# Layer-norm statistics as columns, with routing and replication interleaved

## The reference

```
xn = (x - mean(x)) / sqrt(var(x) + 1e-5)
attn: q, k, v = xn @ w_qkv.T + b; q = silu(q); k = softmax(k, over tokens)
      out = q @ (k.T @ v) per head; out = layernorm(out) * sigmoid(gate(xn)); out @ w_out.T + b_out
ffn:  logits = xn @ Wr.T                  # 8 experts, the two best per token
      w = softmax(top two); a token is dropped where its place in the expert's queue is 769 or more
      out = sum over the two of w * (xn @ We[e])
```

## Time and profile before

| what | before |
|---|---|
| median of 6 runs | 1111.31 us (1108.59 to 1203.64) |
| the profiled execution | 1109.03 us |
| its span on the slowest core (core 5) | 1107.2 us (1102.3 to 1107.2 over the cores) |
| mean granted clock of TensorE | 0.874 on core 5 |
| TensorE busy | 877.2 us, 79% of the span |
| VectorE busy | 462.4 us, 42% |
| ScalarE, GpSimd busy | 103.7 us, 53.8 us |

### The profile page before, as it was taken

The page is one execution under the profiler, slowest core; times in us unless marked ns, Lnnn a source line. Parts: engine busy times, 40 slices in busy tenths (PEclk is TensorE's granted clock), DMA queues, the critical chain, the costliest instruction groups (busy, mean ns, idle before and its releaser), DMA issues.

```text
span 1107.2 us, 11179 instructions; the slowest of 8 cores (1102.3 to 1107.2 us)
## 1 busy us (share of the span) xinstructions
PE 877.2 (79%) x3914; PEld 357.5 (32%) x3914; DVE 462.4 (42%) x700; ACT 103.7 (9%) x123; POOL 53.8 (5%) x50
## 2 busy tenths in 40 slices
PE   1446129999869986415559999999999999999992
PEld 0112003333363331101013344444444444444441
DVE  3547770033320026376763334444444444444441
ACT  1310002210003211402210000000000000000000
POOL 1000000000000000000000000000000000000244
PEclk9768559999959995755559999999999999999996
DMA  4781100050040040000000050405040505050376
GB/s 117 188 154 9 38 1 1 1 77 1 5 73 1 1 68 9 0 0 1 0 0 1 1 77 1 76 1 77 1 76 1 77 1 77 1 76 1 97 245 228
DMA packets 22149, 51.40 MB, mean 46 GB/s; under 512 B 4624, under 2 KB 4624, under 8 KB 21072
## 3 DMA queue, kind: packets, MB, share of 16 engines
q0 software_dynamic: 15008, 25.49, 15.3%
q1 hardware_dynamic: 4208, 12.63, 4.0%
q10 hardware_dynamic: 2880, 12.58, 2.9%
HBM read 67.79 MB, written 8.39 MB: 69 GB/s over the span
## 4 chain that ended last, share of the span: by engine, by line
PE 65%; DVE 19%; DMA 10%; issue 3%; ACT 2%; DVEq 1%; POOLq 0%; POOL 0%; ACTq 0%; SPq 0%
PE PS L167 65%; DVE ar L177 6%; DMA y<-fpool 6%; DVE scr_b L177 5%; DMA fpool<-x_fm 3%; DVE srow L177 3%; DVE reps L177 1%; ACT bpool L184 1%; DVE qrow L177 1%; ACT qrow L184 1%; DVEq L176 1%; DVE crow L177 0%; DVE drow L177 0%; DVE bpool L177 0%; DVE fpool L177 0%
## 5 line engine op out<-in xcount | busy, mean ns | idle before, releaser
L167 PE MATMUL PS<-ar 128*128 128x512 bf16 (+1 forms) x3200 | 705.0, 378 | 21.3 <-DVE ar L177 8.4
L167 PEld LDWEIGHTS PS<-ar 128*128 128x128 bf16 x3200 | 303.3, 100 | 387.0 <-issue 57.5
L177 DVE SCALAR_TENSOR_TENSOR ar<-PS,lc,ar 128x512 bf16<-128x512 f32 x256 | 192.1, 750 | 251.1 <-PE PS L167 251.1
L177 DVE CAST ar<-PS 128x512 bf16<-128x512 f32 x96 | 66.4, 692 | 94.1 <-PE PS L167 90.5
L167 PE MATMUL PS<-ar,ones_c_b 128*1 128x512 bf16 x64 | 22.8, 493 | 51.0 <-ACT bpool L184 50.6
L184 ACT ACTIVATE ar<-PS 128x512 bf16<-128x512 f32 x64 | 38.2, 597 | 94.7 <-PE PS L167 94.7
L167 PE MATMUL PS<-bpool,wg_sb 64*128 64x512 bf16 x32 | 18.7, 584 | 28.3 <-DVE ar L177 28.3
L198 POOL DMA_DIRECT2D ar<-we x8 | 7.0, 873 | 670.3 <-PE PS L167 670.3
L167 PE MATMUL PS<-drow,ones_b 1*128 1x512 bf16 x8 | 4.4, 554 | 44.1 <-DVE crow L177 35.2
L191 POOL TENSOR_TENSOR fpool<-ar,fpool 128x1024 f32<-128x1024 bf16 x16 | 34.2, 2136 | 90.8 <-DVE ar L177 59.7
L167 PE MATMUL PS<-bias_b,ones_b 1*128 1x512 bf16 x96 | 37.3, 389 | 0.0
(11 more groups left out here) (109 smaller groups left out, 300.0 us busy)
## 6 DMA issues: line engine op xcount, KB each, us to landing
ar<-we POOLq DMA_DIRECT2D x8, 2048.0 KB, 17.0
fpool<-x_tm SPq DMA_DIRECT2D x16, 512.0 KB, 4.1
y<-fpool ACTq DMA_DIRECT2D x16, 512.0 KB, 4.2
fpool<-x_fm SPq DMA_DIRECT2D x4, 1024.0 KB, 6.9
fpool<-x_fm ACTq DMA_DIRECT2D x4, 1024.0 KB, 6.4
ar<-wk_t POOLq DMA_DIRECT2D x1, 2048.0 KB, 23.7
ar<-wv_t POOLq DMA_DIRECT2D x1, 2048.0 KB, 17.3
ar<-wq_t POOLq DMA_DIRECT2D x1, 2048.0 KB, 16.9
```

Of the source, the lines that this page charges most:

```text
L167: i = eng.matmul(out, l, r, start=start, stop=stop)
L177: getattr(eng, name)(*a, **k).then_inc(S["dv"], 1)
```

## The change

Three new tiles: a 128x128 identity in bf16 (`ident_b128`, one more DMA on POOL's queue, ahead of the biases and the weights) and two `[128, 16]` bf16 tiles `rb_c` and `nmb_c`.

The row arithmetic of lines 287 to 312 goes. In its place TensorE first turns `srow` and `qrow` themselves into columns, in fp32, and the mean, variance, root and reciprocal are computed on `[128, 16]`. To get the rows back for the replication, the two column tiles are transposed by a matmul with the identity to `[16, 128]`, copied to SBUF, and two DMAs on SP's queue flatten them to `drow` and `crow` on one partition. All of this stands between the routing matmuls in program order: the columns ahead of chunk 0, the transposes and the DMAs ahead of chunk 2, the replication ahead of chunk 4.

```
+                w("tensor", "dv", t_stats_ev)
+                for tc in range(NT):
+                    mm(bank(4)[:, tc:tc + 1], srow[0:1, 128 * tc:128 * (tc + 1)],
+                       ones_c_f[0:1, 0:1], start=True, stop=True)
...
+                w("vector", "pe", t_cols_pe)
+                dve("tensor_scalar_mul", dsc[:], bank(4)[:, 0:NT], 1.0 / D, inc=False)
+                t_ce = dve("tensor_scalar_mul", nv1c[:], bank(4)[:, NT:2 * NT], 1.0 / D)
...
+                t_mu2 = act("activation", w0c[:], dsc[:], AF.Square)
...
+                t_csd = act("activation", v0c[:], w1c[:], AF.Sqrt, bias=eps_sb[:, 0:1])
+                w("vector", "ac", t_csd)
+                dve("reciprocal", r_c[:], v0c[:], inc=False)
+                dve("tensor_copy", rb_c[:], r_c[:], inc=False)
...
                 for h in range(HC):
+                    if h == 2:
+                        w("tensor", "dv", t_colmath)
+                        w("tensor", "d2", t_ltri)
+                        mm(bank(5)[0:16, 0:128], rb_c[:, :], ident_b128[:, :],
+                           start=True, stop=False)
+                        mm(bank(5)[0:16, 128:256], nmb_c[:, :], ident_b128[:, :],
+                           start=False, stop=True, inc=True)
...
+                        t_stg = dve("tensor_copy", bpool2[0:16, 0, 0:256],
+                                    bank(5)[0:16, 0:256])
+                        w("sync", "dv", t_stg)
+                        dma("d1", drow[0:1, :], bpool2[0:16, 0, 0:128])
+                        t_rows_dma = dma("d1", crow[0:1, :], bpool2[0:16, 0, 128:256])
+                    if h == 4:
+                        w("tensor", "d1", t_rows_dma)
+                        for which, rowsrc in ((0, drow), (1, crow)):
+                            for tb in range(TB):
...
                     for tb in range(TB):
                         sl = slice(512 * tb, 512 * (tb + 1))
                         mm(bank(tb)[0:8, :], wr_hi[:, h, :], xhi[:, h, sl],
...
-                dve("tensor_scalar_mul", crow[:], srow[:], 1.0 / D, inc=False)
-                t_mu1 = dve("tensor_scalar_mul", drow[:], qrow[:], 1.0 / D)
...
-                dve("reciprocal", srow[:], qrow[:], inc=False)
-                t_r_bf = dve("tensor_copy", drow[:], srow[:])
-                w("tensor", "dv", t_r_bf)
...
-                t_reps_toks = []
-                for which, rowsrc in ((0, drow), (1, crow)):
```

More of the change, by code:

```diff
@@ L70, in build_nc @@
         ident_bf = sb("ident_bf", [8, 8], BF16)
+        ident_b128 = sb("ident_b128", [128, 128], BF16)
+        rb_c = sb("rb_c", [128, NT], BF16)
+        nmb_c = sb("nmb_c", [128, NT], BF16)
         ones_b = sb("ones_b", [128, 512], BF16)
@@ L211, in program @@
                 dma("d2", ltri_sb[:], ltri)
+                dma("d2", ident_b128[:], ident)
                 t_ltri = dma("d2", ident_bf[:], ident[0:8, 0:8])
@@ L274, in program @@
                              wr_hi[:].rearrange("p c e -> p (c e)"), ALU.subtract)
+                w("tensor", "dv", t_stats_ev)
+                for tc in range(NT):
+                    mm(bank(4)[:, tc:tc + 1], srow[0:1, 128 * tc:128 * (tc + 1)],
+                       ones_c_f[0:1, 0:1], start=True, stop=True)
+                for tc in range(NT):
+                    mm(bank(4)[:, NT + tc:NT + tc + 1], qrow[0:1, 128 * tc:128 * (tc + 1)],
+                       ones_c_f[0:1, 0:1], start=True, stop=True, inc=(tc == NT - 1))
@@ new lines, in program @@
+                t_cols_pe = c["pe"]
+                w("vector", "pe", t_cols_pe)
+                dve("tensor_scalar_mul", dsc[:], bank(4)[:, 0:NT], 1.0 / D, inc=False)
+                t_ce = dve("tensor_scalar_mul", nv1c[:], bank(4)[:, NT:2 * NT], 1.0 / D)
+                w("scalar", "dv", t_ce)
+                w("scalar", "gp", t_const_gp)
+                t_mu2 = act("activation", w0c[:], dsc[:], AF.Square)
+                w("vector", "ac", t_mu2)
+                t_cvar = dve("tensor_tensor", w1c[:], nv1c[:], w0c[:], ALU.subtract)
@@ new lines, in program @@
+                w("scalar", "dv", t_cvar)
+                t_csd = act("activation", v0c[:], w1c[:], AF.Sqrt, bias=eps_sb[:, 0:1])
+                w("vector", "ac", t_csd)
+                dve("reciprocal", r_c[:], v0c[:], inc=False)
+                dve("tensor_copy", rb_c[:], r_c[:], inc=False)
+                dve("tensor_scalar_mul", nmu_c[:], dsc[:], -1.0, inc=False)
+                dve("tensor_tensor", w1c[:], dsc[:], r_c[:], ALU.mult, inc=False)
+                t_colmath = dve("tensor_scalar_mul", nmb_c[:], w1c[:], -1.0)
@@ L275, in program @@
                 w("tensor", "dv", t_wrlo)
                 w("tensor", "d2", t_wrhi)
+                t_rows_dma = None
+                t_reps_toks = []
                 for h in range(HC):
+                    if h == 2:
[5 more added lines that the diff above has]
+                           start=False, stop=True, inc=True)
+                        t_rowsT_pe = c["pe"]
+                        w("vector", "pe", t_rowsT_pe)
+                        t_stg = dve("tensor_copy", bpool2[0:16, 0, 0:256],
[7 more added lines that the diff above has]
+                            for tb in range(TB):
+                                if t_reps_toks:
+                                    w("tensor", "dv", t_reps_toks[-1])
+                                mm(bank(7)[:, :], ones_b[0:1, 0:128],
+                                   rowsrc[0:1, 512 * tb:512 * (tb + 1)],
+                                   start=True, stop=True, inc=True)
+                                tk = c["pe"]
+                                w("vector", "pe", tk)
+                                t_reps_toks.append(
+                                    dve("tensor_copy",
+                                        reps[:, which, 512 * tb:512 * (tb + 1)],
+                                        bank(7)[:, :]))
@@ L295, in program @@
-                t_sd = act("activation", qrow[:], srow[:], AF.Sqrt, bias=eps_sb[0:1, 0:1])
-                w("vector", "ac", t_sd)
-                dve("reciprocal", srow[:], qrow[:], inc=False)
-                t_r_bf = dve("tensor_copy", drow[:], srow[:])
-                w("tensor", "dv", t_r_bf)
[L300 to L312, removed]
-                t_reps_toks = []
-                for which, rowsrc in ((0, drow), (1, crow)):
[L316 to L328, removed]
@@ L356, in program @@
                 w("tensor", "d2", t_ltri)
-                w("tensor", "dv", t_cols_ev)
+                w("tensor", "dv", t_colmath)
                 for tc in range(NT):
@@ L402, in program @@
                 t_d = dve("tensor_tensor", dsc[:], v0c[:], nv1c[:], ALU.add)
-                w("gpsimd", "dv", t_r_bf)
+                w("gpsimd", "pe", t_cols_pe)
                 t_offz = gps("memset", offr[0:1, 0:E], 0.0)
```

## The result

The changed kernel took 1120.65 us (median of 14 runs) against 1111.13 us before (31 runs): ratio 1.0085, 95% interval 1.0072 to 1.0098, that is 9.4 us (8.0 to 10.9) slower. It moved the way that was forecast, and somewhat further than the 8.2 us of the sum. In some executions, the profiled one of the changed kernel among them, the cores of one die stood at a lower clock (there 0.788 to 0.791 against 0.866 to 0.871) and took longer (1206.0 to 1212.4 us against 1112.1 to 1116.8); the ratio leaves these executions out, and all lines of the changed kernel are those of core 7, the slowest core of the other die (span 1116.8 us).

A forecast was written before the change was run, and what follows sets the result against it. VectorE's row arithmetic with its 12.95 us reciprocal bounded the stretch before `xn`; without it TensorE's serial work delays `xn` by 9.7 us, less 1.5 for the other queue: +8.2 on 1109.03, 1117 us, range 1108 to 1122.

The forecast's parts named there:

- the sum: Whole kernel: +9.7 us on the path and -1.5 from the other queue, +8.2 us on the profiled 1109.03 us.
- The mark: VectorE's first `xn` operation, at 123.54 us before; forecast at 133.2, +9.7 us, moving the end by the same amount.
- fp32 columns: TensorE ahead of chunk 0: 32 fp32 matmuls in two passes each, low clock, 0.44 us each, 14.1 us.
- routing of chunks 0 and 1: 24 TensorE matmuls after the columns, starting at the low clock: 7 x 0.417 + 17 x 0.216 = 6.6 us.
- transposes, rows by DMA beside chunks 2 and 3: Ahead of the replication: two row DMAs of 2.2 us, level with 24 routing matmuls; TensorE waits about 0.2 us.
- replication, to the next matmul: Eight trips ahead of chunk 4, gaps unfilled: seven intervals of 1.59 us and one of 0.42, 11.6 us.
- routing of chunks 4 to 7 and the hop: 48 TensorE matmuls behind the replication, slow start, 11.8 us, then a 0.18 us hop to VectorE.
- logits: Three steps on the logits after the last routing matmul, just before the first `xn` operation; unchanged at 6.83 us.
- the rival of late rows: Row DMAs run into weight loads and TensorE waits at chunk 4; up to +7 us, 1119 to 1124, chance 0.13.
- The rival of cheap columns: The fp32 column stream reaches the high clock, or its passes do not follow the clock; 1108 to 1113 us, chance 0.25.
- The faster outcome: Second rival, whose description the text given leaves out; 1103 to 1107 us, chance 0.07.
- The term of the other queue: Identity DMA on POOL's queue starts `wk` 2 to 5 us later, helping the last input loads; -1.5 us (0 to -3).

The follow-up runs named there:

- The experiment at the higher clock: Changed kernel with 26 more routing-like matmuls, results unread, before the fp32 columns so these begin at the high clock; 1122.17 us, ratio 1.007 to the kernel before.

## Why the prediction was right

The mechanism was the one forecast: the reciprocal had been the cover of the routing, and with the reciprocal gone TensorE's own work became the path. The mark was put at 56.9 us behind the last `qrow` copy and came at 57.8 on core 7 and at 56.5 on the three other cores of its die. By its steps, predicted and measured on core 7:

| step | predicted us | measured us |
|---|---|---|
| start behind the last copy | 0.25 | 0.15 |
| fp32 columns | 14.1 | 13.7 |
| routing of chunks 0 and 1 | 6.6 | 7.6 |
| transposes, rows by DMA beside chunks 2 and 3 | 5.5 | 5.4 |
| replication, to the next matmul | 11.6 | 11.2 |
| routing of chunks 4 to 7 and the hop | 12.1 | 12.9 |
| logits | 6.8 | 6.8 |

The columns were the term with the widest bounds (6.4 to 16.6), and the two choices in it held: the low clock, and a pass that takes twice as long there. Before the change no run shows a stream of fp32 matmuls, and that it would stand at the low clock was my estimate; the changed kernel showed it at 0.50 from 75.30 to 89.01 us. The fp32 matmul costs 0.428 us, close to the 0.44 taken. The experiment at the higher clock shows that the level set it: 0.112 us a pass at 1.00 against 0.213 at 0.50.

The row DMAs were 1.8 us apart instead of 2.2, and TensorE waited 0.1 us for them; the rival of late rows did not come. The rival of cheap columns fell with the granted clock of 0.50 and the 13.7 us that the columns took. The faster outcome, 1103 to 1107 us, did not come either: TensorE stood idle for 1.01 us before each replication matmul but the first, and the granted clock from 102 to 113 us was 0.60.

Two terms were short on this core. Each slow start lasted some eleven matmuls (89.01 to 93.66 us and 113.21 to 117.81) and not the seven of the earlier trace rows: 1.0 us too little for chunks 0 and 1 and about 0.9 for chunks 4 to 7. Together they are more than the difference of the two marks; columns and replication, which came out 0.4 shorter each, made up for the rest. On the other three cores the slow starts were shorter (chunks 0 and 1 took 6.8 us), so the seven of the earlier trace rows were one case of a number that varies.

The term of the other queue had about the right size, 1.9 us (0.8 to 3.0) where 1.5 were taken, but not the reason that was given. The two cores of the earlier trace rows do not stand for the eight: in the same trace core 2 issued `wk` first of all, at 35.76, and its copies of the statistics were the first too, at 66.28. And `wk`, put 2 to 5 us later, started in the changed kernel anywhere from 3.5 us earlier to 13.5 us later on the same core, 4.4 in the mean. What the trace of before does show is a small DMA on that queue that takes longer while the DMA engines are busy: the next one waited 5.83 us for the 2 KB of `bk` at a DMA share of 0.89 and 1.74 us for the 2 KB of `bv` at 0.02, though 3.15 us for `bo` at 0.01. That the size fits is luck as far as the runs show.

The sum of 1117 was made on the profiled execution's 1109.03 us, 2.1 us under the median of all runs before. That is most of the 3.7 us to 1120.65; the longer path less the larger gain of the identity's DMA accounts for 0.5, and the last 1.1 us are within the interval of the ratio.

## What to carry to other kernels

When a long operation on one engine is removed, list what other engines did under it: that work can be the next path, as it was here, and the gain is then the removed time less all of it: 28 us of row arithmetic went, and the path grew from 47.3 to 57.8 us. Where nothing independent stood behind a round trip between TensorE and VectorE, it cost its whole length here, 1.4 to 1.6 us; between the routing matmuls the same eight trips cost 0.40 us each. Look at the type of many small matmuls: 32 of one column took 13.7 us in fp32 and 0.9 in bf16, both at a granted clock of 0.50.

## What was not expected of the hardware

One more small DMA ahead of a large weight load made the kernel faster, 1.9 us (0.8 to 3.0), by a way that the traces leave open. And the granted clock fell from 1.00 (84 to 86 us) to 0.51 (88 to 90 us) in the middle of an unbroken stream of fp32 matmuls with one column, in which TensorE showed as busy throughout.
